# One-core transformer block: weights laid out on the host, split into high and low parts beside the work

## What is computed

```python
# A: attention, 16 heads of 64, every product rounded to fixed point (make_fxp: clip, trunc(v * 4096) / 4096)
qkv = einsum('bnd,ed->bne', layernorm(x), w_qkv)           # w_qkv is (3 * 1024, 256)
dots = make_fxp(einsum(q, k) * scale); attn = make_fxp(softmax(dots))
x = x + make_fxp(einsum('bne,de->bnd', make_fxp(attn @ v), w_proj) + b_proj)
# B: cross attention to ctx_512 (16, 128, 128), no fixed point
x = x + softmax((q @ Wq)(ctx @ Wk) * scale) @ (ctx @ Wv) @ Wo + bo
# C: two experts over the same wi_w (1024, 256) and wo_w (256, 1024), each with its own LoRA of rank 16
inter = relu(h @ wi_w.T + (h @ A.T) @ Bm.T); x = x + sum_k top_v[k] * inter @ wo_w.T
```

## Time and profile before

| | before |
|---|---|
| runs | 731.83, 730.24, 731.88 us; median 731.83 us |
| span of the profiled execution | 730.2 us, 1.6 us less than the median of the runs |
| PE busy | 672.8 us (92%) |
| DVE busy | 550.0 us (75%) |
| ACT busy | 413.7 us (57%) |
| POOL busy | 272.6 us (37%) |
| DMA | 18.75 MB in all, most of it in the first 20 us and from 48 to 60 us |

### The profile page before, as it was taken

The page is one execution under the profiler, slowest core; times in us unless marked ns, Lnnn a source line. Parts: engine busy times, 40 slices in busy tenths (PEclk is TensorE's granted clock), DMA queues, the critical chain, the costliest instruction groups (busy, mean ns, idle before and its releaser), DMA issues.

```text
span 730.2 us, 15676 instructions
## 1 busy us (share of the span) xinstructions
PE 672.8 (92%) x5186; PEld 551.7 (76%) x5186; DVE 550.0 (75%) x1142; ACT 413.7 (57%) x1443; POOL 272.6 (37%) x610
## 2 busy tenths in 40 slices
PE   5998879989998899878989999999999889999997
PEld 4777768777886788766777877787788777888986
DVE  5879887887888789757767776677667668787775
ACT  4677756767776777764455455445544563433432
POOL 1166754454445534535354344234333532010110
PEclk9999999999999999999999999999999999999999
DMA  9135100000000000050000000000000000000000
GB/s 312 49 111 150 60 30 1 1 1 1 0 0 0 0 0 0 0 153 1 1 2 16 1 1 1 14 0 0 0 0 0 0 1 1 2 30 0 29 29 29
DMA packets 17002, 18.75 MB, mean 26 GB/s; under 512 B 2851, under 2 KB 15427, under 8 KB 16963
## 3 DMA queue, kind: packets, MB, share of 16 engines
q1 hardware_dynamic: 15330, 15.11, 6.4%
q0 software_dynamic: 1632, 3.15, 1.5%
HBM read 16.16 MB, written 2.10 MB: 25 GB/s over the span
## 4 chain that ended last, share of the span: by engine, by line
PE 35%; POOL 7%; DVE 6%; ACT 3%; issue 3%; DVEq 0%; POOLq 0%; ACTq 0%
PE bank L405 9%; PE bank L407 8%; PE bank L406 8%; POOL p_f L363 6%; PE bank L583 3%; ACT e_sb L889 2%; PE bank L595 2%; PE bank L607 1%; DVE mx L1164 1%; PE bank L729 1%; PE bank L741 1%; DVE bn_st L966 1%; DVE oT_lo L1206 1%; POOL p_int L316 0%; DVE v_sb L1137 0%
## 5 line engine op out<-in xcount | busy, mean ns | idle before, releaser
L363 POOL TENSOR_SCALAR p_f<-e_sb,rsum 128x128 f32<-128x128 f32 x256 | 95.6, 398 | 156.7 <-DVE rsum L1199 156.7
L316 POOL TENSOR_SCALAR p_int<-e_sb,rsc 128x128 int16<-128x128 f32 x256 | 116.2, 475 | 6.3 <-issue 5.7
L889 ACT ACTIVATE e_sb<-bank,neg_max 128x128 f32<-128x128 f32 x256 | 90.1, 380 | 12.1 <-DVE neg_max L1168 11.9
L804 ACT ACTIVATE sgn<-bank 128x512 bf16<-128x512 f32 x96 | 57.2, 598 | 57.6 <-PE bank L407 57.6
L819 ACT ACTIVATE e_sb<-si 128x128 f32<-128x128 int16 x256 | 75.1, 303 | 0.0
L1021 DVE SCALAR_TENSOR_TENSOR ri<-sgn,bank 128x512 int16<-128x512 bf16 x96 | 62.5, 677 | 7.3 <-ACT sgn L804 6.5
L875 ACT COPY q_sb<-bank 128x512 f32<-128x512 f32 x32 | 18.8, 587 | 84.5 <-PE bank L407 84.5
L311 POOL TENSOR_TENSOR rsc<-rsum,growth 128x8 f32<-128x8 f32 x32 | 6.7, 209 | 156.0 <-DVE rsum L1047 156.0
L889 ACT ACTIVATION_READ_ACCUMULATOR e_sb<-bank,neg_max 128x1 f32 x256 | 55.9, 218 | 0.0
L405 PE MATMUL bank<-xnT_hi,wqkvT_lo 128*128 128x512 f32 x128 | 53.6, 419 | 2.2 <-DVE ri L1021 1.3
L1175 DVE COPY aT_sb<-bank 128x512 f32<-128x512 f32 x64 | 41.2, 685 | 12.7 <-PE bank L583 12.5
(11 more groups left out here) (162 smaller groups left out, 2039.5 us busy)
## 6 DMA issues: line engine op xcount, KB each, us to landing
x_sb<-in_x SPq DMA_DIRECT2D x4, 512.0 KB, 10.3
wqkv_raw<-in_L_attn_w_qkv SPq DMA_DIRECT2D x2, 1024.0 KB, 10.2
out<-x_sb SPq DMA_DIRECT2D x8, 256.0 KB, 2.2
wqkv_raw<-in_L_attn_w_qkv SPq DMA_DIRECT2D x2, 512.0 KB, 5.1
wp_raw<-in_L_attn_w_proj SPq DMA_DIRECT2D x1, 1024.0 KB, 12.3
raw_b<-in_L_xattn_Wq SPq DMA_DIRECT2D x2, 512.0 KB, 3.3
wq_hi<-in_L_xattn_Wq POOLq DMA_DIRECT2D x2, 512.0 KB, 4.1
wo_hi<-in_L_xattn_Wo POOLq DMA_DIRECT2D x2, 512.0 KB, 8.4
```

What stands on the lines that cost most here:

```text
L316: i = nc.gpsimd.tensor_scalar(p_int[:, t, :], e_sb[:, t, :], rsc[:, t:t + 1], -0.5, ALU.mult, ALU.add)
L363: i = nc.gpsimd.tensor_scalar(p_f[:, t, :], e_sb[:, t, :], rsum[:, t:t + 1], 0.0, ALU.mult, ALU.add)
L804: nc.scalar.activation(sgn[:, m % 2, :], proj_ps[m % 2][:, :], ACT.Sign).then_inc(a_sgn, 1)
L889: last = nc.scalar.activation(e_sb[:, t, :], s_ps[hh][:, (t % 4) * P:(t % 4 + 1) * P], ACT.Exp, bias=neg_max[:, t:t + 1], scale=DH ** -0.5 ...
```

## The change

The host lays out the weights and the context so that the contracted dimension is on the partitions, and all transposes of weights and context leave the kernel, with the ACT and DVE work that went with them. The raw copy of a weight is loaded into the place of its low part.

- Queues of the first loads. SP loads `x` of group 0 as four DMAs of 128 KiB, then qkv pieces for slots 2 to 7 (256 KiB each), among them the second half of v (512 KiB) and `w_proj` (1 MiB), then the bias, the rest of `x` (1.5 MiB), two small tensors and the raw weights of B (3 MiB) in one DMA. ACT issues q and k of slot 0, the first half of v, and q and k of slot 1. POOL issues casting DMAs for all other high parts.
- High parts: ACT copies q and k of slot 0 and the first half of v; all others come by casting DMA on POOL's queue (3.25 MiB for A, 3 MiB for B, 2 MiB for C).
- Low parts: DVE computes the first; POOL computes all others by `tensor_tensor`. For A these are numbered 1 to 11: numbers 1 to 5 ahead of slot 0, 6 to 8 behind slot 0, then one behind each of slots 1 to 3. POOL works in order, and the first `p_int` follows behind number 8. PE waits for each by `w_lo`. For B six pieces of 128x1024 move to slots 3 and 6 of groups 1 to 3 of A. For C four pieces of 128x1024 and the LoRA tiles come in slots 1 to 7 of group 0 of B.
- The scale `FIX * GROW` moves into `rstd`: `inv_std` gets one more small product in A (`units`).
- PE's q block at the head of a group of B no longer waits for the context; the v block does.
- DVE still waits in slot 1 of group 0 for the bias and all of `x`.

```diff
+            for b in range(GB):
+                sp.dma_start(x_sb[:, b, :], x[b]).then_inc(ld_x0[b], 16)
+            for s in range(2, NP):
+                sp.dma_start(wqk_raw[:, s, :, :, :], wqk[:, s, :, :, :]).then_inc(ld_qk[s], 16)
+                if s == 2:
+                    sp.dma_start(wv_raw[:, 1, :, :], wv[:, 1, :, :]).then_inc(ld_v[1], 16)
+                if s == 3:
+                    sp.dma_start(wp_raw[:, :, :], wp).then_inc(ld_wp, 16)
+            sp.dma_start(bias_a[:, :], b_proj.partition_broadcast(P)).then_inc(ld_b, 16)
             for g in range(1, G):
+                load_x(g)
...
+            sp.dma_start(wB_raw[:, :, :], wB).then_inc(ld_wB, 16)
...
+            def make_low(n):
+                raw, hi, lo, raw_in, hi_in = low_part(n)
+                if n == V_LOW[0]:
+                    pool.wait_ge(w0_hi, 2)
+                else:
+                    pool.wait_ge(raw_in, 16)
+                    pool.wait_ge(hi_in, 16)
+                nc.gpsimd.tensor_tensor(lo, raw, hi.bitcast(F32), ALU.subtract).then_inc(w_lo, 1)
+
+            load_high(2)
...
+            for n in (3, 4, 5, 6):
+                load_high(n)
...
+            inv_std(0, scaled=True)
+            for n in (1, 2):
+                make_low(n)
+            for n in (7, 9):
+                load_high(n)
+            for n in (3, 4, 5):
+                make_low(n)
...
             for s in range(NP):
                 a_slot(0, s, first=True)
+                for n in ((10, 11), (), (), (), (), (), (), ())[s]:
+                    load_high(n)
+                for n in ((6, 7, 8), (9,), (10,), (11,), (), (), (), ())[s]:
+                    make_low(n)
                 if s == 3:
+                    nc.gpsimd.dma_start(wB_hi[:, :, :], wB).then_inc(lh_wB, 16)
...
+                if not first and s in (3, 6):
+                    chunk = 2 * (g - 1) + (s - 3) // 3
...
+                    nc.gpsimd.tensor_tensor(lo, raw, hi.bitcast(F32), ALU.subtract).then_inc(wB_done, 1)
...
             for s in range(NP):
                 b_slot(0, s, first=True)
...
+                if s in (1, 2):
...
+                    nc.gpsimd.tensor_tensor(wi_lo[:, s - 1, :], wi_raw[:, s - 1, :], wi_hi[:, s - 1, :].bitcast(F32),
+                                            ALU.subtract).then_inc(cw_lo, 1)
+                if s in (3, 4):
...
+                    nc.gpsimd.tensor_tensor(wd_lo[:, half, :], wd_raw[:, half, :], wd_hi[:, half, :].bitcast(F32),
+                                            ALU.subtract).then_inc(cw_lo, 1)
...
+                if s in (6, 7):
...
+                    nc.gpsimd.tensor_scalar(lb_raw[:, :], lb_raw[:, :], lora_sign[:, 1 - k:2 - k], 0.0, ALU.mult,
+                                            ALU.add).then_inc(g_lb, 1)
+                    pool.wait_ge(g_lb, 3 + 3 * k)
+                    nc.gpsimd.tensor_copy(lbT[:, :], lb_raw[:, :]).then_inc(g_lb, 1)
+                    pool.wait_ge(g_lb, 4 + 3 * k)
+                    nc.gpsimd.tensor_tensor(lbT[64:96, :], lb_raw[64:96, :], lbT[64:96, :].bitcast(F32),
+                                            ALU.subtract).then_inc(g_lb, 1)
...
             for s in range(2):
                 b_slot(G, s, drain=True)
-                if s == 0:
-                    pe.wait_ge(g_lb, 10)
-                    pe.wait_ge(b_e, NP * G)
-                c_weights(C_PARTS[s])
...
+            for s in range(2):
+                nc.scalar.dma_start(wqk_raw[:, s, :, :, :], wqk[:, s, :, :, :]).then_inc(ld_qk[s], 16)
+                if s == 0:
+                    nc.scalar.dma_start(wv_raw[:, 0, :, :], wv[:, 0, :, :]).then_inc(ld_v[0], 16)
+
+            for count, n in enumerate((QK_LOW[0], V_LOW[0])):
+                raw, hi, _, raw_in, _ = low_part(n)
+                act.wait_ge(raw_in, 16)
+                nc.scalar.copy(hi, raw).then_inc(w0_hi, 1)
...
+            raw, hi, lo, _, _ = low_part(0)
+            dve.wait_ge(w0_hi, 1)
+            V.tensor_tensor(lo, raw, hi.bitcast(F32), ALU.subtract).then_inc(w0_lo, 1)
             norm_apply(0, 0, (ln_T, 0))
...
                 if first and s == 1:
                     dve.wait_ge(ld_b, 16)
-                    dve.wait_ge(ld_xr, 16 * (G - 1))
+                    for loaded in ld_x[1:]:
+                        dve.wait_ge(loaded, 16)
```

More of the change, by code:

```diff
@@ L74, with build @@
 BLOCKS = block_index(8)
-def build(nc, x, ctx, w_qkv, w_proj, b_proj, Wq, Wk, Wv, Wo, bo, wi_w, wo_w, lora_As, lora_Bs,
-          top_i, top_v, out):
+def build(nc, x, ctxT, wqk, wv, wp, b_proj, wB, bo, wiT, wdT, lora_AT, lora_BT, top_i, top_v, out):
     place, mem = sbuf_map(nc)
@@ L407, in split3 @@
                 return pe.matmul(out_, wh, mh, start=False, stop=last, **kw)
[L409 to L430 removed]
+            pe.wait_ge(g_const, 6)
             def normed_T(n, prev_reads):
@@ L507, in a_slot @@
                 base = block_index(s)
-                a_block(g, base, s * P, True)
-                a_block(g, base + 1, E + s * P, True)
-                if first and s in (1, 2):
-                    a_weights_T(PREP_PARTS[s + 1])
-                if first:
-                    wait(pe, w_lo, (10, 0, 12, len(PREP), 0, 0, 0, 0)[s])
+                if first and s > 0:
+                    wait(pe, w_lo, QK_LOW[s])
+                for i in range(2):
+                    a_block(g, base + i, [w[:, s, :, i, :] for w in (wqk_hi, wqk_lo)], True)
                 lag2 = not (first and s < 2)
@@ L516, in a_slot @@
                     a_transpose(n - 2)
+                if first and s == 3:
+                    wait(pe, w_lo, WP_LOW[1])
                 if not (first and s < 3):
-                    project_out(n - 3, (s - 3) % NP, a_olo, a_pj, (wpT_hi, wpT_lo), (a_z, 2 * g))
+                    project_out(n - 3, (s - 3) % NP, a_olo, a_pj, (wp_hi, wp_lo), (a_z, 2 * g))
                 if s == NP - 1:
@@ L526, in a_slot @@
                     a_attend(n - 2, p, BLOCKS * gg + (block_index(1) + 4 if p < 4 else block_index(3) + 4))
+                if first and s in (0, 2):
+                    wait(pe, w_lo, V_LOW[s // 2])
                 if s < 4:
@@ L616, in b_slot @@
                 lag2 = not (first and s < 2) and not (drain and s >= 2)
-                if s == 0 and not drain:
-                    wait(pe, ld_ctx, 16 * (g + 1))
-                    wait(pe, ln_lo, 2 * (G + g) + 1)
-                    for b in range(GB):
-                        last = pe.transpose(one_ps[:, b * P:(b + 1) * P], ctx_sb[:, b, :], ident[:, :])
-                    last.then_inc(b_cT, 1)
                 def transposes():
@@ L729, in up @@
                     pe.matmul(u[:, :], lb1T[:, s * P:(s + 1) * P], lowT[:, :], start=False, stop=True).then_inc(c_u, 1)
-                if first and s == 2:
-                    wait(pe, cw_lo, len(C_PREP))
                 if not drain and s > 0:
@@ L832, in a_slot @@
                 sign_of(g, base + 1)
-                if first and s in (1, 2):
-                    a_weights_high(PREP_PARTS[s + 1])
                 lag2 = not (first and s < 2)
```

434 lines of the change are left out of this document (188 added, 246 removed).

## The result

| | before | after |
|---|---|---|
| time, median us (range, runs) | 731.04 (730.22 to 731.88, 4) | 738.51 (736.88 to 741.04, 4) |
| ratio, 95% interval | | 1.011 (1.0086 to 1.0135) |
| span of the profiled execution, us | 730.2 | 739.2 |
| its own time, us | about 731.8 | 741.04 |
| DMA moved, MB | 18.75 | 24.51 |

The kernel is 1.1% slower. The forecast was 723.7, range 716 to 730: wrong in sign. The profiled execution of after is the slowest of its four, 2.5 us above their median, so its rows add up to 9.0 us more span, not to 7.5.

What follows compares the result with a forecast made beforehand. The kernel was taken as mostly PE in long blocks, with short ACT, DVE and POOL loops in some slots. Terms 2.6 + 0 + 4.3 + 0.4 - 3.2 + 4.0 = 8.1 us took 731.8 to 723.7, range 716 to 730.

Steps and rivals of the forecast that it cites:

- Start to slot 2: From the first loads to slot 2 of A: 2.6 us gained, with bounds of 0 to 6.5.
- at 1 to 2 us of DVE: Slots 0 and 1 of A: POOL's low parts hold DVE up by 1 to 2 us, overlapping the wait for x.
- I take 6.1: Start of A: the first x lands at 6.1 us, between 3.6 alone and 6.5 at a third of the rate.
- The rest of group 0 of A: Slots 3 to 7, B's six low parts moving to groups 1 to 3: balance 0, from 1 gained to 2 lost.
- The wait for Wo: Wait for the last piece of B's weights, in A: it goes, gaining 4.3 us (3.5 to 4.8).
- Head of B: Heads of B's groups: PE's wait for cT_lo behind four transposes goes, gaining 0.4 us in all (0 to 1).
- Group 0 of B: First group of B: POOL's four extra pieces and LoRA work lose 3.2 us (1 to 6.5).
- The low parts hold the DVE for another 0.3: Group 0 of B: POOL's low parts hold DVE up, costing 0.3 us of the 3.2 lost.
- The LoRA term: Slot 6 of group 0 of B: 5.7 us of LoRA work against 3.52 idle, losing 2.2 us (0 to 5.1).
- B to C: Between B and C: weight transposes and waits of 5.2 us leave, less 1.2 for the lower clock, gaining 4.0.
- The one that ended on the slow side: Start: loads at 234 GB/s complete x at 43, stalling DVE, POOL and PE 13 us more; 736.5 us, chance 0.06.
- Rival 1: LoRA work and port at their upper bounds: group 0 of B loses 6.5, A's low parts 2; 729.0 us, chance 0.12.

Runs made afterwards that it cites:

- e1_xn_first: The kernel after, with POOL's first low part held back until DVE has written the four xn, all DMAs unchanged: 734.88 us, ratio 1.0051.
- e5_wp_later: The kernel after, with POOL's low parts held until xn is written and w_proj's two low parts moved out of slot 0: 730.43 us, ratio 1.0003.
- e2_before_pool4: The kernel before, with four unused 128x1024 POOL subtractions added behind the first rstd and no DMA added: 736.13 us, ratio 1.0079.

## Why the prediction was wrong

**Start to slot 2 (-2.6 forecast, +7.6 measured).** The first failed step, and the largest, is the sentence that put POOL's low parts "at 1 to 2 us of DVE", ended under a wait for `x` at 30.2. The row for it was there: 2.03 in place of 0.42. I sized the hold as a few operations in slots 0 and 1 and never asked what DVE does in the very moment in which POOL has five subtractions queued. POOL starts on them as soon as `rstd` is out, and `rstd` is just what DVE's `xn` waits for: the two engines were released by the same event. The hold at `xn` alone was 9.0 us (10.37 against 1.38), with nothing behind it to hide it. The Trainium skill (SBUF — State Buffer, section "SBUF: two separate sides") has the loser of the port pair blocked for a whole instruction, which gives this sign. I had put a loss "if all 18 us did so on the path" in the text, but gave a loss of that size no rival and no chance.

A second term of the same stretch failed: "I take 6.1" for the landing of the first `x`. Its four batches landed one by one, and the last statistics began at 9.37, later than the 6.5 that I had as the worst. With the steps up to `rstd` 0.5 us longer than before, `xn` would have been ready at 13.7, not at 11.0: so it was in e1_xn_first, where nothing held it, and the first product came at 17.26 against my 14.6. The first product of after, 11.7 us later than forecast, is these 2.7 and the 9.0 of the hold.

The other terms of this stretch held. The whole of `x` landed at 30.8, as I had it (30.2), and was no limit, since the bias step came only at 40.55 and stood behind no wait. The first product came 3.4 us behind the transposes, and PE did run its first products at half speed, 0.43 us apart until 30.67 and 0.24 from 31.10. That is 4.8 us from the first one at 26.27, against my 4.6.

```profile
40.55 0.29 DVE L1067 TENSOR_SCALAR bias_a<-bias_a 128x256 f32<-128x256 f32 x1
```

**The rest of group 0 of A (0), and the moved parts.** Measured -0.5, and +0.8 over groups 1 to 3, inside my "from 1 gained to 2 lost".

**The wait for Wo (-4.3).** Measured -4.2. The difference of two neighbouring slots in a group with and one without the wait was the right way to price it.

**Head of B (-0.4).** Measured +0.7, with 6.8 us of lower clock behind it (before had 3.4). In e5_wp_later the same code passed without such a stretch at -1.8. The term was small, and its sign hung on a clock stretch that moved from kernel to kernel.

**Group 0 of B (+3.2 forecast, +7.2 measured).** Two terms of the sum were mis-sized. "The low parts hold the DVE for another 0.3" was 3.2 us by the time of slot 4 (from +4.4 to +7.7 in after; 0.9 when cut in pieces): the loop through `mx`, `neg_max` and the exponentials has its tiny operation right behind `p_f`, where POOL takes up the next subtraction. I priced the hold by the size of these operations and not by POOL's. The 0.7 of slot 4 was right (+7.7 to +8.5 by slot 6). The LoRA term was 2.2 and came to 3.1 (+8.5 to +11.6), but not as I had it: its own length was 4.9 us (392.87 to 397.74, with the waits between), under my 5.7, and the `p_f` behind it started 9.83 later than the one of before (398.99 against 389.16), so only 1.3 us of it is overrun. The `p_f` itself took 3.25 in place of 2.82, which is 0.4; and the last 1.3 us came behind it, where PE had stood for 3.07 us and its granted clock was at the lower level from 403.2 for 3.4 us. I had taken a price for the clock at the start and at C, and none here.

**B to C (-4.0).** Measured -3.4, with 6.8 us at the lower level, for which I had taken 1.2 us off. Its rows, PE behind the last `p_f`, answer to the earlier trace rows:

```profile
606.55 2.82 POOL L381 TENSOR_SCALAR p_f<-e_sb,rsum 128x128 f32<-128x128 f32 x8 [4.46 <-DVE rsum L1168]
...
609.42 1.97 PE L621 MATMUL bank<-ident,p_f 128*128 128x128 f32 x8 [3.69 <-POOL p_f L381]
```

The eight transposes took 1.97 in place of 1.09: PE stood 3.69 without work, as I had written.

**The rivals.** The one that ended on the slow side was the wrong mechanism: a starved start at 234 GB/s. The windows 12 to 24 and 24 to 32 moved 398 and 401 GB/s, above the 347 of the earlier trace rows.

```profile
12.00:24.00 12.00, 1.17 (x6) 1.20 (x7) 10.54 (x5) 0.04 (x1) 11.90 (x12) 1.00 1.08 398
24.00:32.00 8.00, 6.51 (x19) 4.93 (x18) 2.07 (x3) 2.19 (x4) 4.73 (x3) 1.00 1.13 401
```

(The columns are busy us and counts of PE, its weight loads, DVE, ACT and POOL, then the granted clock, the DMA share and GB/s.) In the first window DVE is "busy" 10.54 of 12 us with five operations beside POOL's 11.90, and PE has 1.17: a stall that looks like work. The clock column reads 1.00 in both although the products lie 0.43 apart up to 30.67, so in this trace the level of the start is read from the products. Rival 1 named the port and the LoRA work, but at 2 us more in A and 3.3 more in B, where the hold took 9.0 at the start alone and B came out 4.0 worse. The sum itself adds up; of the chances, those for a faster kernel give 0.88 by the list, not 0.87.

## What to carry to other kernels

When work moves to POOL, ask for each of its instructions which VectorE operation starts beside it, and charge that operation up to the whole POOL instruction, and more if POOL has several back to back; the size of VectorE's own operation is no guide (0.28 us became 2.54). It costs most where one event releases both (here `rstd`) and where a tiny operation stands in a loop of waits (here `neg_max`). The same work placed behind VectorE's critical step, cut in short instructions, and dealt out in portions smaller than POOL's idle time of that very slot, together with a wait of PE cut to the half that it reads, turned 1.1% slower into 0.9% faster.

## What the runs showed of the hardware that I had not expected

- **A VectorE operation can be held over several POOL instructions.** One `xn` of 0.4 us took 6.46 beside three subtractions, one `q_sb` took 5.22 beside eight pieces of 256 columns, while in e2_before_pool4 VectorE got through one `xn` with each of four subtractions (1.98 each). What decides between the two was not found. The Trainium skill (SBUF — State Buffer, section "SBUF: two separate sides") gives the lock for one instruction; these two rows show more than that.
- **Not every VectorE operation is held.** Beside the same subtractions `xnT_lo`, which reads PSUM, took 0.69 (at 24.58 in after, beside 24.06 to 28.73 on POOL), as it does alone.
- **The issue of a casting DMA cost POOL about the same at every size.** In after it took 0.54 to 0.78 us at 256 KiB and 0.64 at 1 MiB and at 3 MiB; for the last I had allowed 5.
- **Shorter instructions cost POOL a fifth to a third more.** Four of 256 columns took 2.8 to 3.1 us in place of 2.35; where VectorE got in between them its part fell by more (7.68 to 2.56 for the four `xn`).
